# Masked keys by strided transfers through DRAM in every stacked attention

## The chip, the cores and the metric

One of the cores of a Trainium2 chip runs the whole program; seven stand idle. The metric is the device time in microseconds of one execution, the median of three. The engines, as the profile names them: PE multiplies matrices (PEld loads its weights), DVE, ACT and POOL work on vectors, SP only issues transfers. DMA engines, 16 for the core, carry the transfers, and semaphores order everything.

## The reference

`x` is 64 sequences of 128 tokens of width 128; the context has 120 tokens per sequence. Four layers, each a cross attention and a feed-forward block:

```python
x = x + _L0_xattn_ref(_layernorm(x), ctx, ctx, pad, ...)     # a0: every 4th key per head
x = x + _L0_ffn_ref(_layernorm(x), ...)                      # f0
x = x + _L1_xattn_ref(_layernorm(x), ctx, wq, bq, ...)       # a1: plain
x = x + _L1_ffn_ref(_layernorm(x), ...)                      # f1
x = x + _L2_xattn_ref(_layernorm(x), ctx, ctx, mask, ...)    # a2: mask; routing for f2 beside it
x = x + _L2_ffn_ref(_layernorm(x), ...)                      # f2
x = x + _L3_xattn_ref(_layernorm(x), ctx, ctx, ...)          # a3: causal, no biases
x = x + _L3_ffn_ref(_layernorm(x), ...)                      # s3 and f3
# inside _L3_ffn_ref:
h = layernorm(x, ln1_scale, ln1_shift)
x = x + attention(h, wq, wk, wv, wo, bo)                     # s3: causal self attention, 128 keys
```

Every attention has 16 heads of width 8:

```python
q = (x_q @ wq + bq); k = (x_kv @ wk + bk); v = (x_kv @ wv + bv)    # split into 16 heads
scores = einsum('bhqd,bhkd->bhqk', q, k) / sqrt(8)
out = einsum('bhqk,bhkd->bhqd', softmax(scores + mask), v) @ wo + bo
```

## The kernel before

`attention_phase` is called once per attention (a0, a1, a2, a3, s3). The trace calls the tiles of a0 to a3 `a_...` and those of s3 `s_...`. A block works on 16 groups of four sequences. All but a0 are "packed" (stacked): 16 slots per group, slot = 4 x sequence + unit, where a unit is four heads. In a slot PE multiplies 96 rows of stacked queries with 96 rows of stacked, masked keys into scores for four heads (L1276; in a2, a3 and s3 the mask is added by L1282), DVE takes the row maxima (L991) and subtracts them (L996), ACT takes the exponential (L1172). Three slots later PE turns the result (L1291), ACT copies it (L1178), and four to six slots later PE multiplies it with the values (L1315), DVE inverts the sums and normalises (L1004, L1010), PE applies Wo (L1330). PE takes its work in the order of the program: scores of the slot, what is behind, and in some slots a projection for the next group (`slot_of`: keys in slot 0, normalised rows 4, queries 7 or 8, values 13; in s3, whose keys come out of its own rows, rows 1, keys 4, queries 8, values 13).

"Stacked" means three float32r terms for full precision: the keys as high, low, high part in partitions 0 to 31, 32 to 63, 64 to 95 (32 dimensions of one unit each), the queries as high, high, low. "Masked" means: the unit's four heads share these 32 dimensions, so the keys stand four times side by side, each copy with zeros in the dimensions of the three other heads. The way of the keys of a group through a1, a3 and s3: PE projects them (L1245), ACT evicts them (L1164 or L1166) and rounds the high part (`high_part`, L1130), POOL subtracts for the low part (`low_part`, L882), SP stacks them by twelve transfers of 32 partitions into K3 (`stack_terms`, L791), POOL multiplies each of the four units of K3 with `slots`, the 0/1 table of heads (`masked_keys`, L723), into KM. The queries then go by twelve transfers into QR (L797). SP issues in order, and after the keys it waits for the low part of the queries. PE waits for each unit's KM and QR in the slots of the first sequence (`scores`).

a2 goes another way: `place_keys` writes the three terms to the DRAM tensor `stacked_keys` (L805), SP waits until they are there (`keys_kept`), and four strided reads (L812) put each head's eight dimensions at their places in a KM whose zeros were written once at the start (L911) and by group 0's masked keys; then `stack_queries` (L821). Its Wk, Wq and biases are brought into another order of dimensions at the start of the block: weights by ACT (`reorder`, L1117), biases by transfers (`dims_first`, L696).

There are two KM and two QR, one K3, one high and one low part for keys and queries.

Of the kernel before, what the change touches and what calls it, by code (L numbers as in the profile page):

```python
# [22 lines left out]
P = 128  # L23
D = 128
# [563 lines left out]
def attention_phase(nc, R, I, name, wq, wk, wv, wo, bq=None, bk=None, bv=None, bo=None, hepos=False,  # L588
# [20 lines left out]
    with ExitStack() as stack:  # L609
# [63 lines left out]
        if packed:  # L673
# [3 lines left out]
            q3_in = [sem(n_(f"q3_in{i}")) for i in range(4)]  # L677
        if route:
            keys_kept, keys_empty, keys_in = (sem(n_(s)) for s in ("keys_kept", "keys_empty", "keys_in"))
            reordered = sem(n_("reordered"))  # L680
# [6 lines left out]
        n_weights += 3 * bool(route)  # L687
        n_weights += 2 * (ln is not None) + hepos
# [3 lines left out]
        def dims_first(eng, col, bias, there):  # L692

            by_dim = bias.rearrange("(i j r a) -> i r j a", i=4, j=4, a=1)
            for i in range(4):
                eng.dma_start(cols[32 * i:32 * i + 32, col:col + 1], by_dim[i],  # L696
                              allow_slow_non_contiguous=True).then_inc(there, 16)

# [34 lines left out]
        with nc.Block() as block:  # L733
            @block.sync
            def _(sp):
# [4 lines left out]

                sp.dma_start(PT[0][:, 0:D] if route else Wk[:], wk).then_inc(keys_first_in, 16)
                if not route:
                    if bk is not None:
                        sp.dma_start(cols[:, 1:2], bk.rearrange("(p a) -> p a", a=1)).then_inc(keys_first_in, 16)
                    sp.dma_start(slots[:], I["slots" if packed else "slot_classes"]).then_inc(keys_first_in, 16)
                if not own_keys:
                    ctx_load(0, 0)
                for t, w in ((PT[0][:, D:2 * D] if route else Wq[:], wq), (Wv[:], wv), (Wo[:], wo)):
                    sp.dma_start(t, w).then_inc(weights_in, 16)
                if route:  # L750
                    dims_first(sp, 0, bq, weights_in)
                for c, v in ((0, None if route else bq),) + (((3, ln[0]), (4, ln[1])) if ln else ()):
                    if v is not None:
                        sp.dma_start(cols[:, c:c + 1], v.rearrange("(p a) -> p a", a=1)).then_inc(weights_in, 16)
# [17 lines left out]
                def stack_first():  # L772
# [7 lines left out]
                    for i in (2, 3):  # L780
                        for term, part in enumerate((HIGH, HIGH, LOW)):
                            sp.dma_start(QR[0][32 * term:32 * term + 32, i, :].bitcast(F32),
                                         part["q"][32 * i:32 * i + 32, :].bitcast(F32)).then_inc(q3_in[i], 16)

                def stack_terms(g, par):
# [7 lines left out]
                    sp.wait_ge(low_ready["q"], g + 1)  # L793
                    for i in range(4):
                        at_least(sp, sc_ready, (g - 2) * S + (GB - 1) * U + i + 1)
                        for term, part in enumerate((HIGH, HIGH, LOW)):
                            sp.dma_start(QR[par][32 * term:32 * term + 32, i, :].bitcast(F32),  # L797
                                         part["q"][32 * i:32 * i + 32, :].bitcast(F32)).then_inc(q3_in[i], 16)

                def place_keys(g, par):  # L800

                    sp.wait_ge(low_ready["k"], g + 1)
                    for term, part in enumerate((HIGH, LOW, HIGH)):
                        kept = R.keys.rearrange("(t q i f) -> t i q f", t=3, q=32, i=4)[term]
                        sp.dma_start(kept, part["k"][:].bitcast(F32)).then_inc(keys_kept, 16)  # L805
# [4 lines left out]
                    of_head = R.keys.rearrange("(q j s k) -> j q s k", q=24, j=4, k=KN)  # L810
# [4 lines left out]
                def stack_queries(g, par):  # L815
# [13 lines left out]
                if own_keys:  # L829
                    groups_loop(sp, lambda g, par, first, last: stack_first() if first else stack_terms(g, par), 3)  # L830
                    return
# [8 lines left out]
                stack_first()  # L840
                if route:
                    for g in range(1, NG):
                        if g + 1 < NG:
                            ctx_load(g + 1, (g + 1) % 2)
                        place_keys(g, g % 2)
                        stack_queries(g, g % 2)
                    return

                def pair(g):
                    ctx_load(g + 2, 0)  # L850
                    stack_terms(g + 1, 1)
                    ctx_load(g + 3, 1)
                    stack_terms(g + 2, 0)

                pairs_loop(sp, NG - 2, pair)
                stack_terms(NG - 1, 1)

            @block.gpsimd
            def _(pool):
# [32 lines left out]
                def prepare(g, par):  # L892
                    low_part("k", g)
                    if not route:
                        masked_keys(pool, nc.gpsimd, g, par, (0,))
                    scatter(g - 1, 4, 7)
                    low_part("q", g)
                    if not route:
                        masked_keys(pool, nc.gpsimd, g, par, (1, 2, 3))
                    scatter(g - 1, 15, 3)  # L900
# [7 lines left out]
                low_part("k", 0)  # L908
                masked_keys(pool, nc.gpsimd, 0, 0, (0, 2))
                if route:  # L910
                    nc.gpsimd.memset(KM[1][:].bitcast(F32), 0.0).then_inc(keys_empty, 1)  # L911
                    route.spares()
# [192 lines left out]
            def _(act):  # L1105
                a = nc.scalar
                if route:
                    dims_first(act, 1, bk, keys_first_in)
                    by_dim = I["slots"].rearrange("(t j r) w -> t r j w", t=3, j=4)
# [10 lines left out]

                if route:
                    reorder(Wk, 0)
# [75 lines left out]
                for step in steps_of:  # L1198
                    if step == "v" and bv is None:
                        act.wait_ge(prep_pool, 2)  # L1200
                    if step == ("ht" if own_keys else "q"):
                        act.wait_ge(weights_in, 16 * n_weights)
                        at_least(act, prep, n_prep)
                    if route and step == "ht":
                        act.wait_ge(weights_in, 16 * n_weights)
                        reorder(Wq, 1)
# [16 lines left out]
            def _(pe):  # L1223
# [140 lines left out]

                if route:
                    pe.wait_ge(reordered, 1)
# [6 lines left out]
                for step in steps_of[1:]:  # L1373
                    if route and step == "q":
                        pe.wait_ge(reordered, 2)
# [1261 lines left out]
def build(nc, I, out):  # L2637
    with ExitStack() as stack:
# [9 lines left out]
        R.dispatched = nc.dram_tensor("dispatched", [E2 * CAP + 2 * NB * P, ROW], F32).ap()  # L2648
        R.keys = nc.dram_tensor("stacked_keys", [3 * P * GB * KC], F32).ap()
        R.chosen = nc.dram_tensor("chosen", [2 * NB * P + SPARE, D], F32).ap()  # L2650
# [115 lines left out]
```

## Time and profile before

| | us |
|---|---|
| median of 3 runs | 4092.15 |
| lowest, highest | 4079.58, 4092.81 |
| the profiled execution, device time | 4094.84 |
| its span in the trace | 4093.0 |
| PE, DVE, ACT, POOL busy | 3449.9, 3381.5, 2376.4, 1347.5 |
| granted TensorE clock, mean | 0.912 |

The blocks with stacked attention stand at about 549 to 990 us (a1), 1372 to 1965 (a2), 2407 to 2890 (a3) and 2911 to 3430 (s3). The profile is of one execution. A share of busy time over the span mixes stages; a row of one stage says more. "Idle before" is the time for which the engine had nothing to do before the instructions of a group, with what ended it. The duration of a transfer issue (SPq) is only the issue; the landing is seen in the DMA share or in who waited for it.

### The profile page before, as it was taken

What the parts mean: (1) busy time and instruction counts of PE and PEld (TensorE: products, weight loads), DVE (VectorE), ACT (ScalarE), POOL (GpSimd) and SP (SyncE); (2) the same over time, 40 slices, a digit from 0 to 9 for tenths busy, and PEclk for the clock granted to TensorE, in tenths of its full rate; (3) what the DMA queues carried; (4) which work ended last, traced back from release to release, by engine and by line L of the source; (5) the groups of instructions that cost most, each with busy time, mean ns of one, the idle gap of its engine ahead of it and who ended that gap; (6) DMA issues with size and microseconds to landing.
All of it is one profiled execution on the core that took longest, in us unless ns stands there. A gap on an engine that the chain in (4) does not pass through costs nothing. (4 is left out here: it accounts for less than half of the span.)

```text
span 4093.0 us, 94365 instructions
## 1 busy us (share of the span) xinstructions
PE 3449.9 (84%) x31907; PEld 2493.3 (61%) x31907; DVE 3381.5 (83%) x6484; ACT 2376.4 (58%) x4442; POOL 1347.5 (33%) x876
## 2 busy tenths in 40 slices
PE   6983979999499698888568839999499998899999
PEld 3543647676477465566446627777366666677777
DVE  7888879999799798777655569999788887788888
ACT  2431647777277466666545527777567664566665
POOL 1210025554000202222344435564255552122222
PEclk9995979999599799999789869999699997899999
DMA  2001312221100133332122142222222222000000
GB/s 65 14 23 54 145 45 68 62 65 44 55 1 0 43 86 79 79 81 73 46 85 61 57 127 64 65 67 52 76 48 54 55 50 83 18 16 15 15 11 15
DMA packets 182176, 221.18 MB, mean 54 GB/s; under 512 B 59144, under 2 KB 131148, under 8 KB 178957
## 3 DMA queue, kind: packets, MB, share of 16 engines
q1 hardware_dynamic: 172277, 198.88, 17.8%
q0 software_dynamic: 8192, 16.92, 1.5%
q8 instruction: 189, 3.10, 0.3%
q10 hardware_dynamic: 1432, 1.58, 0.2%
q14 instruction: 86, 0.70, 0.1%
HBM read 64.15 MB, written 53.26 MB: 29 GB/s over the span
## 5 line engine op out<-in xcount | busy, mean ns | idle before, releaser
L1172 ACT ACTIVATE a_p<-a_p 128x480 f32<-128x480 f32 x832 | 501.6, 603 | 453.9 <-DVE a_p L996 442.8
L991 DVE TENSOR_REDUCE a_mx<-a_sc 128x4 f32<-128x480 f32 (+1 forms) x832 | 539.9, 649 | 142.4 <-PE a_sc L1282 89.1
L1178 ACT ACTIVATE a_pt<-a_tp 120x512 f32<-120x512 f32 x832 | 485.3, 584 | 110.7 <-PE a_tp L1291 102.9
L996 DVE TENSOR_TENSOR a_p<-a_sc,a_mx 128x480 f32<-128x480 f32 x832 | 531.0, 638 | 19.7 <-DVE a_mx L991 0.5
L1291 PE MATMUL a_tp<-ident,a_p 128*120 128x128 f32 x3328 | 516.7, 278 | 19.3 <-issue 12.0
L1291 PEld LDWEIGHTS a_tp<-ident,a_p 128*120 128x120 f32 x3328 | 411.0, 140 | 98.6 <-issue 51.0
L723 POOL TENSOR_TENSOR a_km<-a_k,a_slots 96x1920 fp32r<-96x1920 f32 x126 | 426.6, 3405 | 133.3 <-DMA a_k<-a_kh 133.3
L1276 PE MATMUL a_sc<-a_km,a_qr 96*128 96x480 f32 x768 | 401.1, 522 | 64.6 <-DVE a_p L996 48.8
L1315 PE MATMUL a_nd<-a_pt,a_vm 120*32 120x128 f32 x6656 | 304.4, 286 | 27.4 <-ACT a_pt L1178 24.6
L2276 ACT ACTIVATE f_s<-f_pu 128x512 f32<-128x512 f32 x256 | 153.3, 599 | 214.0 <-PE f_pv L1758 214.0
L1315 PE MATMUL a_nd<-a_pt,a_dm 120*32 120x128 f32 x6656 | 271.0, 276 | 1.1 <-issue 1.1
L1276 PEld LDWEIGHTS a_sc<-a_km,a_qr 96*128 96x128 f32 x768 | 148.2, 193 | 170.8 <-issue 95.8
L1004 DVE RECIPROCAL a_rd<-a_nd 128x128 f32<-128x128 f32 x256 | 242.5, 947 | 10.6 <-PE a_nd L1315 10.3
L723 POOL TENSOR_TENSOR s_km<-s_k,s_slots 96x2048 fp32r<-96x2048 f32 x62 | 223.6, 3625 | 55.2 <-DMA s_k<-s_kh 55.2
L1172 ACT ACTIVATE s_p<-s_p 128x512 f32<-128x512 f32 x256 | 161.2, 630 | 138.2 <-DVE s_p L996 138.0
L2187 DVE TENSOR_TENSOR f_a<-f_s,f_pv 128x512 f32<-128x512 f32 x256 | 175.2, 685 | 77.4 <-ACT f_s L2276 70.7
L1315 PEld LDWEIGHTS a_nd<-a_pt,a_vm 120*32 120x32 f32 x6656 | 146.8, 110 | 143.0 <-issue 71.4
L2199 DVE TENSOR_TENSOR f_al<-f_a,f_ah 128x512 fp32r<-128x512 f32 x256 | 228.9, 894 | 0.0
L2162 POOL TENSOR_TENSOR f_ya<-f_ya,f_yg 128x512 f32<-128x512 f32 x96 | 124.8, 1300 | 302.7 <-DVE f_yg L2212 302.5
L991 DVE TENSOR_REDUCE s_mx<-s_sc 128x4 f32<-128x512 f32 x256 | 175.0, 684 | 44.7 <-PE s_sc L1282 43.4
L1282 PE MATMUL a_sc<-a_addm,ident_bf 128*128 128x480 bf16 x512 | 199.7, 390 | 0.7 <-issue 0.7
L1315 PEld LDWEIGHTS a_nd<-a_pt,a_dm 120*32 120x32 f32 x6656 | 195.8, 112 | 3.2 <-issue 2.5
(458 smaller groups left out, 8796.1 us busy)
## 6 DMA issues: line engine op xcount, KB each, us to landing
a_qr<-a_qh SPq DMA_DIRECT2D x372, 64.0 KB, 2.0
a_k<-a_kh SPq DMA_DIRECT2D x264, 60.0 KB, 2.0
a_ctx<-in_ctxT SPq DMA_DIRECT2D x64, 240.0 KB, 2.7
a_qr<-a_ql SPq DMA_DIRECT2D x186, 64.0 KB, 2.0
a_km<-stacked_keys SPq DMA_DIRECT2D x60, 180.0 KB
dispatched<-f_empty SPq DMA_DIRECT2D x8, 1040.0 KB, 20.0
f_xr<-dispatched SPq DMA_DIRECT2D x32, 260.0 KB, 2.6
chosen<-f_none SPq DMA_DIRECT2D x8, 1024.0 KB, 11.9
```

The lines of the kernel that those rows point to most:

```text
L723: v.tensor_tensor(KM[par][:, i, :, :].rearrange("p b (j k) -> p b j k", k=KN), K3[:, i, :, :].unsqueeze(2).to_broadcast([TR, GB, 4, KN]), ...
L991: v.tensor_reduce(mx[:], view, AX.X, ALU.max).then_inc(mx_ready, 1)
L996: v.tensor_tensor(PR[s % 4][:].rearrange("p (h k) -> p h k", k=k), view, mx[:].unsqueeze(2).to_broadcast([P, heads, k]), ALU.subtract).the ...
L1004: v.reciprocal(RD[:], ND[bt % 2][:, 1, :]).then_inc(rd_ready, 1)
L1172: a.activation(PR[s % 4][:], PR[s % 4][:], ACT.Exp).then_inc(exp_ready, 1)
L1178: a.activation(PT[s % 4][0:KN, :], TP[s % 2][0:KN, :], ACT.Copy).then_inc(pt_ready, 1)
L1276: last = t.matmul(SC[s % 2][:, 0:W], queries, keys, start=True, stop=not masked)
L1282: last = t.matmul(SC[s % 2][:, 0:W], R.ident_bf[:], addm[:].unsqueeze(1).to_broadcast([P, 4, KN]), start=False, stop=True)
L1291: last = t.transpose(TP[s % 2][0:KN, q * P:(q + 1) * P], PR[s % 4][:, q * KN:(q + 1) * KN], R.ident[:])
L1315: last = t.matmul(ND[j % 2][32 * q:32 * q + 32, what, :], w, PT[s % 4][0:KN, q * P:(q + 1) * P], start=(what == 0 and i == 0), stop=(i == ...
L2187: v.tensor_tensor(A[s % 2][:], S[s % 2][:], PV[s % 2][:], ALU.mult).then_inc(Z["a_ready"], 1)
L2199: v.tensor_tensor(AL[s % 4][:], A[s % 2][:], AH[s % 4][:].bitcast(F32), ALU.subtract).then_inc(Z["lo_ready"], 1)
```

## The change

a1, a3 and s3 go a2's way. `stack_terms` now holds what `place_keys` did, for all; SP's loops are written out in full; POOL no longer runs `masked_keys` after group 0 but clears KM[1] once; PE waits for one count of four reads in slot 0 instead of four counts; weights, biases and slots are loaded and reordered as in a2; `stacked_keys` grows so that it holds 128 keys. a0, a2 and the feed-forward blocks stay.

```diff
-        n_first = 8 if route else 2 + (bk is not None)
+        n_first = 2 + (bk is not None) if hepos else 4 + 4 * (bk is not None)
...
         def parts_free(eng, step, g):
-            if route and step == "k" and g > 1:
-                eng.wait_ge(keys_kept, 48 * (g - 1))
+            if step == "k" and isinstance(g, int) and g == 1:
+                for i in range(4):
+                    eng.wait_ge(k3_in[i], 48)
+            elif step == "k":
+                at_least(eng, keys_kept, 48 * (g - 1))
             else:
                 for i in range(4):
-                    at_least(eng, (k3_in if step == "k" else q3_in)[i], 48 * g)
+                    at_least(eng, q3_in[i], 48 * g)
...
                 def stack_terms(g, par):
                     sp.wait_ge(low_ready["k"], g + 1)
-                    for i in range(4):
-                        at_least(sp, km_ready[i], g)
-                        for term, part in enumerate((HIGH, LOW, HIGH)):
-                            sp.dma_start(K3[32 * term:32 * term + 32, i, :, :].rearrange("p b k -> p (b k)"),
-                                         part["k"][32 * i:32 * i + 32, :].bitcast(F32)).then_inc(k3_in[i], 16)
+                    for term, part in enumerate((HIGH, LOW, HIGH)):
+                        sp.dma_start(kept_keys[term].rearrange("q (i f) -> i q f", i=4),
+                                     part["k"][:].bitcast(F32)).then_inc(keys_kept, 16)
+                    sp.wait_ge(keys_kept, 48 * g)
+                    if par == 1:
+                        sp.wait_ge(keys_empty, 1)
+                    at_least(sp, sc_ready, (g - 1) * S)
+                    for j in range(4):
+                        sp.dma_start(KM[par][j:TR:4, :, :, j * KN:(j + 1) * KN].bitcast(F32),
+                                     of_head[j]).then_inc(keys_in, 16)
                     sp.wait_ge(low_ready["q"], g + 1)
...
                 def prepare(g, par):
                     low_part("k", g)
-                    if not route:
-                        masked_keys(pool, nc.gpsimd, g, par, (0,))
                     scatter(g - 1, 4, 7)
                     low_part("q", g)
-                    if not route:
-                        masked_keys(pool, nc.gpsimd, g, par, (1, 2, 3))
                     scatter(g - 1, 15, 3)
...
                 masked_keys(pool, nc.gpsimd, 0, 0, (0, 2))
+                nc.gpsimd.memset(KM[1][:].bitcast(F32), 0.0).then_inc(keys_empty, 1)
...
                     if packed and j == 0:
-                        if not route or g == 0:
-                            pe.wait_ge(km_ready[i], g + 1)
+                        if isinstance(g, int) and g == 0:
+                            pe.wait_ge(km_ready[i], 1)
                         elif i == 0:
                             pe.wait_ge(keys_in, 64 * g)
                         pe.wait_ge(q3_in[i], 48 * (g + 1))
```

The order on SP in s3, one group, before (s_k is K3, s_kh and s_kl the high and low part of the keys, s_qr the stacked queries):

```order
L791 DMA s_k<-s_kh 32x512
L791 DMA s_k<-s_kl 32x512
L791 DMA s_k<-s_kh 32x512 x2
L791 DMA s_k<-s_kl 32x512
L791 DMA s_k<-s_kh 32x512 x2
L791 DMA s_k<-s_kl 32x512
L791 DMA s_k<-s_kh 32x512 x2
L791 DMA s_k<-s_kl 32x512
L791 DMA s_k<-s_kh 32x512
L797 DMA s_qr<-s_qh 32x512 x2
```

The same place now (stacked_keys is the DRAM tensor, s_km the masked keys):

```order
L793 DMA stacked_keys<-s_kh 4x32x512
L793 DMA stacked_keys<-s_kl 4x32x512
L793 DMA stacked_keys<-s_kh 4x32x512
L800 DMA s_km<-stacked_keys 24x16x128 x4
L806 DMA s_qr<-s_qh 32x512 x2
L806 DMA s_qr<-s_ql 32x512
```

Between the third and the fourth row SP now waits for the three writes, and the first query transfer stands behind the four reads.

The order on POOL in s3 at the start of the block, before (s_ql is the low part of the queries):

```order
L882 TENSOR_TENSOR s_kl<-s_kt,s_kh 128x512
L723 TENSOR_TENSOR s_km<-s_k,s_slots 96x2048 x2
L882 TENSOR_TENSOR s_kl<-s_kt,s_kh 128x512
L723 TENSOR_TENSOR s_km<-s_k,s_slots 96x2048
L882 TENSOR_TENSOR s_ql<-s_qt,s_qh 128x512
L723 TENSOR_TENSOR s_km<-s_k,s_slots 96x2048 x3
```

And now:

```order
L855 TENSOR_TENSOR s_kl<-s_kt,s_kh 128x512
L724 TENSOR_TENSOR s_km<-s_k,s_slots 96x2048 x2
L879 MEMSET s_km 96x8192
L855 TENSOR_TENSOR s_kl<-s_kt,s_kh 128x512
L855 TENSOR_TENSOR s_ql<-s_qt,s_qh 128x512
```

After group 0 only the two low parts stand on POOL, and one clearing of KM[1] ahead of them.

## Rows read from the trace of the kernel before

**Rows 1.** busy time by stage: a1, a3, s3; the first row names the columns
```profile
core 0: us, PE busy (x) PEld busy (x) DVE busy (x) ACT busy (x) POOL busy (x), PEclk, DMA share, GB/s
600.00:985.00 385.00, 365.25 (x5032) 269.66 (x5021) 367.41 (x697) 281.47 (x518) 221.47 (x85) 1.00 0.26 64
2440.00:2880.00 440.00, 437.08 (x5942) 317.02 (x5938) 401.74 (x763) 320.80 (x592) 235.10 (x89) 1.00 0.25 60
2970.00:3400.00 430.00, 407.80 (x5279) 288.14 (x5279) 385.03 (x685) 296.08 (x533) 234.94 (x84) 1.00 0.22 53
```

**Rows 2.** what PE waited for in s3: us in total, times, longest
```profile
PE s_pj L1238 <- DVE s_h L157: 19.0, 14, 2.0
```

**Rows 3.** groups of s3, a3 and a2: busy us, mean ns, idle before
```profile
L723 POOL TENSOR_TENSOR s_km<-s_k,s_slots 96x2048 fp32r<-96x2048 f32 x54 | 193.3, 3597 | 48.2 <-DMA s_k<-s_kh 48.2
L157 DVE TENSOR_SCALAR s_h<-x,s_mean,s_rstd 128x128 f32 x52 | 27.7, 591 | 0.0
...
L996 DVE TENSOR_TENSOR a_p<-a_sc,a_mx 128x480 f32<-128x480 f32 x149 | 94.5, 634 | 1.9
...
L996 DVE TENSOR_TENSOR a_p<-a_sc,a_mx 128x480 f32<-128x480 f32 x193 | 123.1, 638 | 2.8 <-issue 0.3
```

**Rows 4.** L157 in s3: ns shortest, median, longest
```profile
L157 DVE TENSOR_SCALAR s_h<-x,s_mean,s_rstd x52: 332/334/1952, 2998.7 to 3370.1; 128x128 f32 x52
```

**Rows 5.** SP in a2 by start; two stretches of it; landing (us)
```profile
1446.07 0.59 SPq L805 DMA_DIRECT2D stacked_keys<-a_kh  x1
1457.08 3.26 SPq L812 DMA_DIRECT2D a_km<-stacked_keys  x4
1460.45 1.23 SPq L821 DMA_DIRECT2D a_qr<-a_qh  x2
1468.04 0.59 SPq L821 DMA_DIRECT2D a_qr<-a_ql  x1
...
1453.00:1454.00 1.00, 1.00 (x30) 0.66 (x22) 1.00 (x3) 0.98 (x2) 0.00 (x0) 1.00 0.26 102
1465.00:1466.00 1.00, 1.00 (x8) 0.78 (x7) 0.98 (x2) 0.00 (x0) 0.00 (x0) 1.00 0.18 41
...
a_qr<-a_ql SPq DMA_DIRECT2D x186, 64.0 KB, 2.0
```

**Rows 6.** s3 by start: SP, POOL, PE (scores of slots 0, 3, 4)
```profile
2980.98 0.51 SPq L791 DMA_DIRECT2D s_k<-s_kh  x1
3011.55 0.52 SPq L791 DMA_DIRECT2D s_k<-s_kh  x1
...
2984.25 3.60 POOL L723 TENSOR_TENSOR s_km<-s_k,s_slots 96x2048 fp32r<-96x2048 f32 x1 [3.30 <-DMA s_k<-s_kh]
...
2996.41 0.50 PE L1276 MATMUL s_sc<-s_km,s_qr 96*128 96x512 f32 x1
3002.76 0.47 PE L1276 MATMUL s_sc<-s_km,s_qr 96*128 96x512 f32 x1
3005.28 0.49 PE L1276 MATMUL s_sc<-s_km,s_qr 96*128 96x512 f32 x1
```

**Rows 7.** a1: SP's first key transfer, PE's scores of slots 0 and 3
```profile
613.11 0.51 SPq L791 DMA_DIRECT2D a_k<-a_kh  x1
...
634.73 0.49 PE L1276 MATMUL a_sc<-a_km,a_qr 96*128 96x480 f32 x1
639.24 0.49 PE L1276 MATMUL a_sc<-a_km,a_qr 96*128 96x480 f32 x1
```

**Rows 8.** a2, two stretches of 10 us
```profile
1650.00:1660.00 10.00, 6.39 (x66) 3.65 (x64) 6.44 (x21) 7.01 (x16) 6.35 (x8) 0.99 0.37 77
1660.00:1670.00 10.00, 9.78 (x87) 6.54 (x84) 8.44 (x23) 6.65 (x14) 1.95 (x2) 0.67 0.45 116
```

**Rows 9.** start of a2: SP's transfers of the query bias
```profile
1374.56 3.08 SPq L696 DMA_DIRECT2D a_cols<-in_L_xattn_b_q  x4
```

**Rows 10.** a2: a wait of DVE that nothing in the profile released
```profile
1659.55 0.66 DVE L991 TENSOR_REDUCE a_mx<-a_sc 128x4 f32<-128x480 f32 x1 [3.25 <-remote]
```

More of the change, by code:

```diff
@@ L683, in attention_phase @@
         rd_ready, ct_ready, o_done, x_added = (sem(n_(s)) for s in ("rd_ready", "ct_ready", "o_done", "x_added"))
-        n_first = 8 if route else 2 + (bk is not None)
+        n_first = 2 + (bk is not None) if hepos else 4 + 4 * (bk is not None)
         n_weights = 3 + sum(a is not None for a in (bq, bo, mask, causal, pad)) + (GB if bv is not None else 0)
-        n_weights += 3 * bool(route)
+        n_weights += 3 * (packed and bq is not None)
         n_weights += 2 * (ln is not None) + hepos
@@ L695, in dims_first @@
             for i in range(4):
-                eng.dma_start(cols[32 * i:32 * i + 32, col:col + 1], by_dim[i],
-                              allow_slow_non_contiguous=True).then_inc(there, 16)
+                eng.dma_start(cols[32 * i:32 * i + 32, col:col + 1], by_dim[i], allow_slow_non_contiguous=True).then_inc(there, 16)
         def class_keys(pool, g, par):
@@ L739, in ctx_load @@
                     sp.dma_start(CTX[par][:], I["ctxT"][:, bass.ds(g * GB, GB), :]).then_inc(ctx_in[par], 16)
-                sp.dma_start(PT[0][:, 0:D] if route else Wk[:], wk).then_inc(keys_first_in, 16)
-                if not route:
+                sp.dma_start(PT[0][:, 0:D] if packed else Wk[:], wk).then_inc(keys_first_in, 16)
+                if hepos:
                     if bk is not None:
                         sp.dma_start(cols[:, 1:2], bk.rearrange("(p a) -> p a", a=1)).then_inc(keys_first_in, 16)
-                    sp.dma_start(slots[:], I["slots" if packed else "slot_classes"]).then_inc(keys_first_in, 16)
+                    sp.dma_start(slots[:], I["slot_classes"]).then_inc(keys_first_in, 16)
                 if not own_keys:
                     ctx_load(0, 0)
-                for t, w in ((PT[0][:, D:2 * D] if route else Wq[:], wq), (Wv[:], wv), (Wo[:], wo)):
+                for t, w in ((PT[0][:, D:2 * D] if packed else Wq[:], wq), (Wv[:], wv), (Wo[:], wo)):
                     sp.dma_start(t, w).then_inc(weights_in, 16)
-                if route:
+                if packed and bq is not None:
                     dims_first(sp, 0, bq, weights_in)
-                for c, v in ((0, None if route else bq),) + (((3, ln[0]), (4, ln[1])) if ln else ()):
+                for c, v in ((0, bq if hepos else None),) + (((3, ln[0]), (4, ln[1])) if ln else ()):
                     if v is not None:
@@ L783, in stack_first @@
                                          part["q"][32 * i:32 * i + 32, :].bitcast(F32)).then_inc(q3_in[i], 16)
+                kept_keys = R.keys[0:3 * P * GB * KN].rearrange("(t q s) -> t q s", t=3, q=32)
+                of_head = R.keys[0:3 * P * GB * KN].rearrange("(q j s k) -> j q s k", q=24, j=4, k=KN)
                 def stack_terms(g, par):
                     sp.wait_ge(low_ready["k"], g + 1)
-                    for i in range(4):
-                        at_least(sp, km_ready[i], g)
-                        for term, part in enumerate((HIGH, LOW, HIGH)):
-                            sp.dma_start(K3[32 * term:32 * term + 32, i, :, :].rearrange("p b k -> p (b k)"),
-                                         part["k"][32 * i:32 * i + 32, :].bitcast(F32)).then_inc(k3_in[i], 16)
[L793 to L802, printed above, removed]
                     for term, part in enumerate((HIGH, LOW, HIGH)):
-                        kept = R.keys.rearrange("(t q i f) -> t i q f", t=3, q=32, i=4)[term]
-                        sp.dma_start(kept, part["k"][:].bitcast(F32)).then_inc(keys_kept, 16)
+                        sp.dma_start(kept_keys[term].rearrange("q (i f) -> i q f", i=4),
+                                     part["k"][:].bitcast(F32)).then_inc(keys_kept, 16)
                     sp.wait_ge(keys_kept, 48 * g)
@@ L829, in _ @@
                 if own_keys:
-                    groups_loop(sp, lambda g, par, first, last: stack_first() if first else stack_terms(g, par), 3)
+                    groups_in_full(lambda g, par, first, last: stack_first() if first else stack_terms(g, par))
                     return
@@ L840, in _ @@
                 stack_first()
[L841 to L856, printed above, removed]
+                for g in range(1, NG):
+                    if g + 1 < NG:
+                        ctx_load(g + 1, (g + 1) % 2)
+                    stack_terms(g, g % 2)
             @block.gpsimd
@@ L1106, in _ @@
                 a = nc.scalar
-                if route:
-                    dims_first(act, 1, bk, keys_first_in)
+                if packed:
+                    if bk is not None:
+                        dims_first(act, 1, bk, keys_first_in)
                     by_dim = I["slots"].rearrange("(t j r) w -> t r j w", t=3, j=4)
@@ L1203, in _ @@
                         at_least(act, prep, n_prep)
-                    if route and step == "ht":
+                    if packed and step == "ht":
                         act.wait_ge(weights_in, 16 * n_weights)
@@ L1363, in group @@
                             behind(g, s, par, False)
-                if route:
+                if packed:
                     pe.wait_ge(reordered, 1)
@@ L1373, in _ @@
                 for step in steps_of[1:]:
-                    if route and step == "q":
+                    if packed and step == "q":
                         pe.wait_ge(reordered, 2)
@@ L2648, in build @@
         R.dispatched = nc.dram_tensor("dispatched", [E2 * CAP + 2 * NB * P, ROW], F32).ap()
-        R.keys = nc.dram_tensor("stacked_keys", [3 * P * GB * KC], F32).ap()
+        R.keys = nc.dram_tensor("stacked_keys", [3 * P * GB * P], F32).ap()
         R.chosen = nc.dram_tensor("chosen", [2 * NB * P + SPARE, D], F32).ap()
```

7 lines of the change are left out of this document (1 added, 6 removed).

## The prediction

> **What bounds the kernel now.** I read the busy time by stage first, then the waits, then single groups. A group is four batches, sixteen slots, and each block has 16 groups. In the block a1 (600 to 985 us), the causal block a3 (2440 to 2880) and the self attention s3 (2970 to 3400) PE is busy 365.25 of 385, 437.08 of 440 and 407.80 of 430 us at the full clock, and POOL 221 to 235 us [rows 1]. So these blocks go at TensorE's pace, and POOL, whose work the change takes away, has about 45% of its time free. What matters is whether anything waits for POOL. In s3 the one large wait of PE is for the normalised rows, 19.0 us in 14 groups [rows 2]; none of PE's waits names the masked keys. Hence the removed work can pay only by what it does to other engines, and the added transfers cost only by when they land.
>
> **What is removed.** Per group of a1, a3 and s3: four POOL multiplications, in s3 3597 ns each [rows 3], 14.4 us; in 45 groups about 640 us of POOL. They lie beside PE work and are worth nothing by themselves. Twelve small SP transfers into K3 per group go too. Do they slow DVE? The subtraction L996 takes 634 ns in a3 beside a busy POOL and 638 in a2, which has no masked keys on POOL [rows 3]: no. Only L157 (SBUF to SBUF, one tensor) shows it: 591 ns on the mean in s3, while its fastest and its median are 332 and 334 [rows 3, 4]. In a1 and a3 its slow ones stand at slots 1 and 2, beside POOL's low part of the keys, which stays; PE is 95 to 99% busy there, and I count 0. In s3 they stand in slot 0, beside the last masked keys, and PE waits behind them. Gain there: 4 x (591 - 332) = 1.0 us of PE's 1.36 us (19.0 / 14) per group.
>
> The Trainium skill (GPSIMD Engine Reference, the table at its head) says that GpSimd and VectorE share SBUF interfaces and collide for DVE instructions in a two-port mode or with two SBUF inputs. By that rule also POOL's four multiplications would have cost DVE only at L157, where the trace has it, so an engine that is freed on this scale brings the softmax nothing; a reader who expects the 640 us of POOL to come back in part is told no by both.
>
> **What is added.** Per group: three writes of the stacked keys to DRAM, a wait for them, four strided reads into KM, and only then the twelve query transfers, since all stand on SP's one queue. a2 does exactly this now (slot 0 as a1, 480 values a row), so its rows give the times. From the first write to the first read 11.0 us (1446.07 to 1457.08), while the 16 DMA engines are busy 0.26: about four of them carry it; in the groups at 1502 and 1538 it is 10.8, and I take that. From the first read to the first query transfer 3.37 us, to the last query transfer 10.96 us. Traffic is down to 0.18 of the engines at 1465, 8 us after the first read, with six query transfers in it; I take keys and the first unit's queries as landed 7.4 us after the first read [rows 5]. The floor is 3.37 + 3.3 = 6.7 us, the 3.3 being what three stacked transfers take now from first issue to use, 2980.98 to 2984.25 [rows 6].
>
> **In a1 and a3** the keys are projected in slot 0. The first transfer goes out at 613.11 and the next group's first scores start at 634.73, 21.6 us later [rows 7]. The new chain needs 10.8 + 7.4 = 18.2 us. 3.4 us are left, and the queries of unit 3 (10.8 + 10.96 + 2.0 to land = 23.8 us) are wanted three slots later, at 639.24, 26.1 us. So 0 for these 30 group changes, bounded by a few us of either sign.
>
> **In s3** the keys are projected in slot 4, since they come out of the group's own rows. First transfer 2980.98, next group's first scores 2996.41: 15.4 us, and the same again 30.57 us on [rows 6]. The new chain: 10.8 us, plus 0.5 because 512 instead of 480 values per row take 1/15 more of some 7.4 us of moving, plus 7.4: 18.7 us. PE reaches slot 0 and waits 3.3 us. Everything in PE's order stands behind it (the turns and values of the previous group, the projection of ht), and DVE and ACT run dry after their queue. Then the queries of units 1 to 3 come behind: the last lands 10.96 + 2.0 = 13.0 us after the first read, so slot 3 starts no sooner than 5.6 us after slot 0, and slot 4 2.5 us later (3002.76 to 3005.28), 8.1 us in all. Before it is 8.87 us (2996.41 to 3005.28), PE's wait for L157 inside, so 0.8 us come back here and that gain is used up. Net +2.5 us per group. Bounds: chain 11.3 + 6.7 with L157's whole gain, 18.0 - 15.4 - 1.2 = +1.4; and 12.0 + 7.8 with nothing back, +4.4. With 15 group changes: +37 us (21 to 66).
>
> **The clock.** In a2 five stretches of 10 us with PE busy 6.4 to 7.1 were each followed by one with the granted clock at 0.66 to 0.83, as at 1650 and 1660 [rows 8]. A wait of 3.3 us plus thinner slots gives about 6.5 of 10. One such fall costs (1 - 0.73) x 10 = 2.7 us of full-speed work. What falls on slots 0 to 4 lengthens the group; what falls later only fills the wait. I take under half, 1.2 us: 15 x 1.2 = +18 (0 to 40).
>
> **Start of the blocks.** Weights come unordered and ACT reorders them; biases come in four transfers, slots in three. a2 shows the price: SP's four bias transfers take 3.08 us [rows 9], one about a seventh of it (0.43). In a1 the scores hang on SP's list (bias vectors, bo, then keys), longer by 3.08 less three issues of 0.43: +1.8. In a3 the slots land 1 us after what gates the first projection now: +1. In s3 the norm covers it: 0. The clearing of KM[1] on POOL (one pass over a buffer, by size at most two of the 3.6 us multiplications) stands before the next low part and delays it by about 1 us, where 3.4 us are left. Sum +3 (1 to 8).
>
> **Sum.** The profiled execution took 4094.84 us. 4094.84 + 37 + 18 + 3 = 4153; it lies 2.7 us above the median of the runs, so 4150.
>
> The Trainium skill (DMA: Bandwidth & Descriptors, Specifications) wants pieces of at least 512 bytes and says that below this the DMA reads, modifies and writes. The pieces of a1, a2 and a3 are 120 x 4 = 480 bytes, those of s3 128 x 4 = 512. By it the reads in s3 land sooner than a2's 7.4 us; the issue of the queries (6.7 us) then decides, and the whole would be 0.7 x 15 = 10 us less, 4140. No row before the change has a 512-byte read of this form.
>
> **Rivals.**
> (A) The keys come in time in s3 too: faster. It decides at 15.4 us from first write to last landing; L157's gain of 1.0 us then stays, 15 x 1.0, less 3 at the starts: 4080. For it: s3 has no indirect transfers beside, and PE's waits in a2 name no key. Against: the write alone took 10.8 us in a2's first groups, where there were none either, and a2 has over 21 us.
> (B) The small gains and losses cancel, the landing being just late: 4092. The chain would have to be 2.5 us shorter than in a2.
> (C) Instructions run short. In a2 DVE stood 3.25 us at 1659.55 with its input ready since 1656.3, and PE's transposes came one by one, all during the write to DRAM [rows 10]. It shows in 5 of a2's 15 writes, each with indirect transfers beside. If a third of the writes of a3 and s3 did it: 10 x 3.2 on top, 4182; in all 45 groups +144, 4294. Against: a2's first writes, without indirect transfers, have nothing of it.
> (D) The chain is late in a1 and a3 also. The margin is 3.4 us; each us beyond costs 30 us: 4180. Against: a2 has the same order at hardly more room, and none of PE's waits there names the keys.
>
> **Chances.** Forecast (s3 late, the rest hidden) 0.79, its own range 4115 to 4180; A 0.08; B 0.04; C 0.06; D 0.03. 0.3% is 12 us, about what a measurement here can tell. Faster: A with a little of B, 0.08; within 0.3%: B and the lowest edge of the forecast, 0.06; slower 0.86. The range, 4108 to 4182, leaves out most of A and B and the upper part of C.
>
> **What would show it.** Right: in s3 PE waits about 3 us at each group's first scores, released by a DMA into s_km or s_qr; the group takes 33 to 34.5 us instead of 30.57; the granted clock of s3 falls below 0.97; a1 and a3 keep 27.6 and 27.9 us per group; L157 in s3 nears 0.34 us; POOL is under 20% busy in the three blocks. Wrong: if s3 keeps 30.6 us or less (A), if PE or DVE show idle time that nothing released (C), or if the time between first write and first read in s3 is not 11.3 us.

## The result, and the profile after

The changed kernel takes 4155.8 us (median of 4 executions, 4152.3 to 4159.8), the kernel before beside it 4092.5. The ratio is 1.016, its 95% interval 1.013 to 1.019. The forecast was 4150, range 4108 to 4182, slower with 0.86. The profiled execution took 4152.3, its span is 4150.5.

The lengths of the blocks show where the time went. Each is counted from the first weight transfer of its attention, in us of the span:

| stretch | before | after | difference |
|---|---|---|---|
| a1 and its feed-forward block | 822.6 | 825.7 | +3.1 |
| a2 and its feed-forward block | 1035.6 | 1032.2 | -3.3 |
| a3 up to the start of s3 | 503.5 | 504.8 | +1.3 |
| s3, to its last output product | 518.2 | 576.8 | +58.6 |

The busy time by stage, three rows that answer to [rows 1]; columns: stretch, its length, busy us and instructions of PE, PEld, DVE, ACT, POOL, the granted clock, the DMA share and GB/s:

```profile
600.00:985.00 385.00, 364.70 (x5043) 269.28 (x5043) 365.48 (x695) 281.03 (x516) 34.81 (x28) 1.00 0.34 90
2440.00:2880.00 440.00, 434.24 (x5933) 316.33 (x5931) 400.36 (x764) 320.38 (x590) 36.11 (x29) 1.00 0.32 85
2970.00:3400.00 430.00, 380.36 (x4711) 273.05 (x4711) 331.53 (x614) 265.86 (x475) 31.93 (x25) 0.92 0.26 70
```

POOL falls from 221 to 235 us to 32 to 36 in all three. In a1 and a3 PE, DVE and ACT keep their busy time and the clock stays at full speed: freeing POOL brings nothing. In s3 PE is busy for less of the same 430 us (380.36 against 407.80), at a mean granted clock of 0.92.

What PE waited for in s3 between 2970 and 3400 us, answering to [rows 2]: the wait for L157 is gone, and in its place stands the wait for the masked keys, 3.8 us a time.

```profile
PE s_sc L1246 <- DMA s_km<-stacked_keys: 49.8, 13, 5.0
```

L157 itself, answering to [rows 3, 4], takes 317 ns on the mean instead of 591 now that POOL is free, and its longest is 346 ns instead of 1952:

```profile
L157 DVE TENSOR_SCALAR s_h<-x,s_mean,s_rstd x52: 245/340/346, 2976.1 to 3387.2; 128x128 f32 x52
```

One group of s3, SP and then PE by start time, answering to [rows 5, 6]. The columns are start, duration and instruction, in brackets the wait before it. The PE lines are the scores of slots 0, 1 and 4:

```profile
2989.12 0.58 SPq L793 DMA_DIRECT2D stacked_keys<-s_kh  x1
3000.48 3.26 SPq L800 DMA_DIRECT2D s_km<-stacked_keys  x4
3003.84 1.24 SPq L806 DMA_DIRECT2D s_qr<-s_qh  x2
...
3008.29 0.77 PE L1246 MATMUL s_sc<-s_km,s_qr 96*128 96x512 f32 x1 [3.66 <-DMA s_km<-stacked_keys]
3010.02 0.77 PE L1246 MATMUL s_sc<-s_km,s_qr 96*128 96x512 f32 x1
...
3017.52 0.50 PE L1246 MATMUL s_sc<-s_km,s_qr 96*128 96x512 f32 x1
```

From the first write to the first read it is 11.36 us, from there to the scores of slot 0 7.81, and from slot 0 to slot 4 9.23. The first scores take 0.77 us instead of 0.5. Single microseconds around them show why (columns as above):

```profile
2993.00:2994.00 1.00, 1.00 (x34) 0.80 (x33) 1.00 (x3) 1.00 (x2) 0.00 (x0) 1.00 0.26 100
3006.00:3007.00 1.00, 0.00 (x0) 0.00 (x0) 0.00 (x0) 0.00 (x0) 0.00 (x0) 1.00 0.61 154
3007.00:3008.00 1.00, 0.00 (x0) 0.00 (x0) 0.00 (x0) 0.00 (x0) 0.00 (x0) 0.53 0.56 149
3012.00:3013.00 1.00, 1.00 (x21) 0.91 (x24) 1.00 (x3) 0.33 (x1) 0.00 (x0) 0.50 0.55 129
3015.00:3016.00 1.00, 1.00 (x10) 0.77 (x8) 0.84 (x2) 0.52 (x2) 0.00 (x0) 1.00 0.00 0
```

The first row lies in the write to DRAM, at a DMA share of 0.26. In the second and third all five engines stand. The granted clock falls to 0.5 (1.2 of 2.4 GHz) before the wait is over, and is full again by 3015.

In s3 the keys of fifteen groups are prepared in this way, and slot 0 of all fifteen waits. The means over the 13 of them that lie between 2970 and 3400 us, by the same four marks, with the same 13 before:

| us per group | before, one group [rows 6] | before, mean | after, mean |
|---|---|---|---|
| first transfer to first read | | | 11.33 |
| first read to scores of slot 0 | | | 8.04 (7.66 to 9.19) |
| the two, or first transfer to scores of slot 0 | 15.43 | 15.43 | 19.37 |
| slot 0 to slot 4 | 8.87 | 9.10 (8.85 to 10.54) | 8.68 |
| slot 4 to the next first transfer | 6.27 | 6.27 | 6.10 |
| group | 30.57 | 30.80 | 34.16 |

The group of [rows 6] is one of the short ones: four groups before are longer, up to 32.24 us. So a group grows by 3.4 us on the mean and not by 3.6.

The +58.6 us of s3 have three parts. From the first of the fifteen key transfers to the last it is 430.98 us before and 479.33 after, fourteen groups at 3.45 us more: +48.4. From the last one to the last output product it is +6.1, with the last late arrival in it (4.1) and slots 0 to 4 of the last group, 8.52 us instead of 6.49. The third part is +4.1 between the start of the block and the first of these transfers, and it has nothing to do with late keys. It stands in the first group, beside the clearing of KM[1] on POOL. POOL, then DVE, then PE after the change, and below them the same DVE and PE rows before:

```profile
2936.37 7.00 POOL L879 MEMSET s_km<- 96x8192 f32 x1
2939.10 4.92 DVE L157 TENSOR_SCALAR s_h<-x,s_mean,s_rstd 128x128 f32<-128x128 f32 x4
2944.17 1.09 PE L1208 MATMUL s_pj<-ident,s_h 128*128 128x128 f32 x4 [9.90 <-DVE s_h L157]
...
2939.48 1.10 DVE L157 TENSOR_SCALAR s_h<-x,s_mean,s_rstd 128x128 f32<-128x128 f32 x4
2940.73 1.08 PE L1238 MATMUL s_pj<-ident,s_h 128*128 128x128 f32 x4 [6.08 <-DVE s_h L157]
```

The first two of the four L157 take 4.35 and 4.16 us instead of 0.33 and end within 0.15 us of the clearing; the other two take 0.33 us. In a1 the clearing, from 578.00 to 584.49, has the same neighbour: an L157 that starts at 581.81 takes 2.76 us and ends at 584.57. In s3 PE waits 9.90 us for these L157 instead of 6.08, and slot 2 of the first group starts 34.7 us after the start of the block instead of 30.6.

### The profile page after: what moved, and what is told of

Same layout as the page of the kernel before. It is cut to its first block and busy times, and to the rows that moved or that the text cites. A ratio compares the mean times of both kernels' runs of the same rounds, so it can differ in the third digit from the quotient of the medians.

```text
span 4150.5 us, 93531 instructions
## 1 busy us (share of the span) xinstructions
PE 3458.4 (83%) x31907; PEld 2507.4 (60%) x31907; DVE 3370.6 (81%) x6484; ACT 2382.2 (57%) x4448; POOL 751.2 (18%) x699
## 3 DMA queue, kind: packets, MB, share of 16 engines
q10 hardware_dynamic: 1952, 1.58, 0.2%
## 5 line engine op out<-in xcount | busy, mean ns | idle before, releaser
L973 DVE RECIPROCAL a_rd<-a_nd 128x128 f32<-128x128 f32 x256 | 242.5, 947 | 10.6 <-PE a_nd L1285 10.3
L1148 ACT ACTIVATE s_pt<-s_tp 128x512 f32<-128x512 f32 x256 | 149.9, 586 | 80.8 <-PE s_tp L1261 78.7
L1246 PE MATMUL s_sc<-s_km,s_qr 96*128 96x512 f32 x256 | 141.6, 553 | 62.3 <-DMA s_km<-stacked_keys 57.3
L1724 PE MATMUL f_py<-f_ah,f_wdhi 128*128 128x512 f32 x384 | 181.7, 473 | 0.0
```

What stands on the lines that cost most here:

```text
L973: v.reciprocal(RD[:], ND[bt % 2][:, 1, :]).then_inc(rd_ready, 1)
L1148: a.activation(PT[s % 4][0:KN, :], TP[s % 2][0:KN, :], ACT.Copy).then_inc(pt_ready, 1)
L1246: last = t.matmul(SC[s % 2][:, 0:W], queries, keys, start=True, stop=not masked)
L1724: t.matmul(out, w_hi, a_hi, start=start, stop=False)
```

## The experiments

Each kernel is told by its edit of the changed kernel, if nothing else is said; the diffs are shortened. The ratio is to the kernel before, timed on the same chip, with its 95% interval. Means per group are over the 13 groups of s3 between 2970 and 3400 us where nothing else is said.

**e1: s3 back on K3 and POOL, a1 and a3 changed.**

```diff
+                    if own_keys:
+                        for i in range(4):
+                            at_least(sp, km_ready[i], g)
+                            for term, part in enumerate((HIGH, LOW, HIGH)):
+                                sp.dma_start(K3[32 * term:32 * term + 32, i, :, :].rearrange("p b k -> p (b k)"),
...
```

> The changed kernel with the self attention s3 back on K3 and POOL's multiplications; a1 and a3 stay on the way through DRAM, as do the new loads at the starts of all blocks. Theory (keys land late in s3 alone): the loss is gone, group of s3 back at 30.6 us, 4096 (4088 to 4104). Rival 1 (a1 and a3 carry part of the loss, by their DMA traffic or instruction supply): 4110 or more. Rival 2 (the freed POOL pays in a1 and a3 and s3 only covers it up): below 4085.

4098.8 us, ratio 1.0008 (0.9994 to 1.0022); s3 519.4 us, groups of 30.84. PE waits for L157 as it did:

```profile
PE s_pj L1223 <- DVE s_h L157: 18.4, 13, 2.0
```

So the loss stands in s3, and e1 is as expected. What a1 and a3 pay at their starts is inside this interval. With K3 back, s3 has no clearing either: its first four L157 take 1.10 us together, and slot 2 of its first group starts 30.8 us after the start of the block. In every kernel here that clears KM[1] in s3 it is 34.7 to 35.0 us. No run moves the clearing alone.

**e3 and e8: s3's keys projected one slot later (5), one slot earlier (3).**

```diff
-    slot_of = dict(zip(steps_of, ... (1, 4, 8, 13)))
+    slot_of = dict(zip(steps_of, ... (1, 5, 8, 13)))
```

e8 has 3 in the place of 5.

> The changed kernel with s3's keys projected in slot 5 instead of slot 4, one slot or 1.5 to 1.9 us later. Theory: the wait grows by the same, from 3.7 to 5.4 us, in 15 group changes: +23 to +29, and up to 10 more by the clock: 4179 to 4195. Rival (wait independent of the slot): 4156.

> The changed kernel with s3's keys projected in slot 3 instead of 4, 2.5 us earlier; the eviction of ht, for which slot 2 had to wait 1.36 us, is over by then. Theory: wait of PE for the keys 1.2 us, no fall of the clock: group 30.5 to 30.8, 4094 to 4102. Rival (slot 2's group of 30.66 us is a floor set by something else than ht): the same 30.66 with another wait.

e3: 4179.1, ratio 1.0202 (1.0169 to 1.0236), groups of 35.45 us. The way through DRAM is as long as in the changed kernel (11.32 and 7.86 us); slot 4 to the next first write takes 7.51 instead of 6.10, and the wait grows from 3.8 to 4.70, not quite to the 5.4 expected. e8: 4114.2, ratio 1.0045 (1.0030 to 1.0061), groups of 31.43 where slot 0 still waits (11.33 and 8.13, then 8.63 and 3.34):

```profile
PE s_sc L1246 <- DMA s_km<-stacked_keys: 17.9, 12, 2.1
```

The time follows the distance between projection and first use, as a late arrival demands. e8 missed its expectation of 4094 to 4102. The wait is 1.5 us on the mean and not 1.2, the clock does fall a little (0.98 in the row of the stage), and a group that waits for no key takes 29.73 us (e7 below), where the expected 30.5 to 30.8 leaves 29.3 to 29.6 for it.

**e2: the keys in slot 2.**

```diff
-    slot_of = dict(zip(steps_of, ... (1, 4, 8, 13)))
+    slot_of = dict(zip(steps_of, ... (1, 2, 8, 13)))
```

> The changed kernel with s3's keys projected in slot 2 instead of slot 4, 3.9 us earlier in a group. Theory: PE's wait of 3.7 us at slot 0 shrinks to under 0.5 us, the clock stays at 1.00, and L157's gain shows: group 29.6 to 30.6 us, 4088 to 4103. Rival (the wait is not a matter of how early the keys are asked for, but of the reads or of contention at slot 0): wait and time stay, about 4150.

4105.4, ratio 1.0030 (1.0014 to 1.0047), groups of 30.66 us, granted clock 1.00. No wait for the keys is left, but another one:

```profile
PE s_pj L1215 <- ACT s_ht L1115: 19.0, 14, 1.4
```

The projection now stands one slot behind the turn of the rows it needs, and waits for ACT's copy of them: 1.36 us per group, as much as L157 cost before the change. With it e2 lies a little above its expected 4088 to 4103. A fixed order of PE has a late limit and an early one.

**e5: the wait filled with fourteen matmuls whose result is not used** (all else as in the changed kernel).

```diff
+                    if own_keys and s == 0 and g > 0:
+                        pe.wait_ge(ready["v"], g + 1)
+                        for _ in range(FILLERS):
+                            t.matmul(PJ[:], R.ident_bf[:], addm[:].unsqueeze(1).to_broadcast([P, 4, KN]), start=True,
+                                     stop=True)
```

> The changed kernel with 14 matmuls of 512 columns (bf16, 0.22 us each at full clock, results unused) on PE ahead of s3's first scores of each group, that is inside the wait. Theory (the fall of the clock is a cost of its own, 1.2 us per group): the granted clock of s3 stays near 1.00, the wait row shrinks to 0.6 us, the group goes from 34.1 to 32.9 us, 4138. Rival (what the clock takes is hidden by the wait for the keys anyway): clock back, group still 34.1, 4156. Rival (the fillers themselves delay): above 4160.

4145.1, ratio 1.0122 (1.0089 to 1.0155); s3 566.5 us instead of 576.8, groups of 33.59 instead of 34.16. The row of the stage has the full clock (its PE time contains the fillers):

```profile
2970.00:3400.00 430.00, 410.49 (x4992) 278.41 (x4987) 337.66 (x625) 268.79 (x485) 31.96 (x25) 1.00 0.27 71
```

PE by start time, the fillers and then the scores of slots 0, 2 and 4:

```profile
3008.08 3.20 PE L1236 MATMUL s_pj<-s_addm,ident_bf 128*128 128x512 bf16 x14
3011.68 0.47 PE L1252 MATMUL s_sc<-s_km,s_qr 96*128 96x512 f32 x1 [0.40 <-issue]
...
3016.50 0.50 PE L1252 MATMUL s_sc<-s_km,s_qr 96*128 96x512 f32 x1 [0.19 <-DMA s_qr<-s_ql]
...
3019.75 0.50 PE L1252 MATMUL s_sc<-s_km,s_qr 96*128 96x512 f32 x1
```

Slot 0 to slot 4 takes 7.93 us here on the mean (8.07 in this group) against 8.68: the low clock costs 0.75 us there, 11 us in 15 groups. In all it is 10.3 us by the length of s3, 10.7 by the medians and 14 by the two ratios. The keys come no sooner than without the fillers: slot 0 starts 8.25 us after the first read on the mean (8.04 without them), and 8.45 in the eight groups in which PE is seen to wait for them after the fillers. So the late arrival and not the clock is the cause; the clock is its smaller consequence.

**e4: in s3 the queries ahead of the wait for the writes.**

```diff
+                    if own_keys:
+                        queries(g, par)
                     sp.wait_ge(keys_kept, 48 * g)
```

> The changed kernel with s3's twelve query transfers issued while SP would wait for the writes, ahead of the four reads. Theory: the queries are ready 6 to 7 us after the first write, so the reads start at about 14 instead of 11.4 us, but then nothing stands behind them, slots 1 to 3 are not held back, and the reads land sooner than 7.8 us after their start: 6 us gives a landing at 20 against 19.2 us. Sum near zero, 4145 to 4175. Rival (the queries in the queue are what holds the reads back): landing at 14 + 4.5, a gain, below 4145.

4208.8, ratio 1.0270 (1.0247 to 1.0293), groups of 37.5: a miss, by more than 30 us. `queries` is the wait for the low part and the twelve query transfers. One group by start time, SP and then PE:

```profile
3040.08 0.55 SPq L793 DMA_DIRECT2D stacked_keys<-s_kh  x1
3047.49 1.89 SPq L813 DMA_DIRECT2D s_qr<-s_qh  x2
...
3055.82 3.31 SPq L802 DMA_DIRECT2D s_km<-stacked_keys  x4
...
3062.69 0.79 PE L1253 MATMUL s_sc<-s_km,s_qr 96*128 96x512 f32 x1 [7.02 <-DMA s_km<-stacked_keys]
```

SP's wait for the low part of the queries ends only 7.4 us after the first write; POOL makes it at 3046.19. The twelve issues then take 8.3 us, and the reads start 15.9 us after the first write on the mean instead of 11.3. Less than half of the query transfers fits into the wait for the write. The run has a side result: with no query transfer behind the reads, the keys land 6.69 us after the first read (6.42 to 6.96, 13 groups) instead of 8.04. So the queries issued behind the reads hold the reads up by about 1.3 us, at least by this one comparison.

**e6: s3's three writes of 128 rows as twelve of 32 rows.**

```diff
-                        sp.dma_start(kept_keys[term].rearrange("q (i f) -> i q f", i=4),
-                                     part["k"][:].bitcast(F32)).then_inc(keys_kept, 16)
...
+                        for i in range(4):
+                            sp.dma_start(kept_keys[term].rearrange("q (i f) -> i q f", i=4)[i],
+                                         part["k"][32 * i:32 * i + 32, :].bitcast(F32)).then_inc(keys_kept, 16)
```

> The changed kernel with s3's three writes to DRAM cut into twelve of 32 rows each, so that each can go out on all 16 DMA engines instead of 4. Theory (the write of 11.4 us is long because four engines carry it): issue of twelve at 0.63 us is 7.6 us and 2 us to land, 9.6 us from first write to first read; the wait of PE goes from 3.7 to 2.0 us, with part of the clock's cost: 15 x 1.7 to 2.4, so 4120 to 4132. Rival (the write is bound by something else, DRAM or the receipt): still 11 us or more, 4150 to 4165.

4095.1, ratio 0.9998 (0.9987 to 1.0009), groups of 30.06: better than the 4120 to 4132 expected. SP by start time:

```profile
2993.16 2.63 SPq L798 DMA_DIRECT2D stacked_keys<-s_kh  x4
3000.85 3.31 SPq L805 DMA_DIRECT2D s_km<-stacked_keys  x4
```

One microsecond inside the write:

```profile
2997.00:2998.00 1.00, 1.00 (x33) 0.81 (x32) 1.00 (x3) 0.97 (x2) 0.00 (x0) 1.00 0.54 135
```

First write to first read is 7.69 us in this group and 7.59 on the mean (6.79 to 8.08) instead of 11.33, at a DMA share of 0.54 instead of 0.26. It is now mostly SP's own issuing, which takes 6.4 us in this group. With 3.7 us off the chain the keys come nearly in time: PE still stands 0.5 us on the mean before slot 0 (up to 1.5), which the profile puts down to nothing. The gain at L157 is seen: the group is 0.7 us shorter than before the change (30.06 against 30.80).

The Trainium skill (DMA: Bandwidth & Descriptors, Why a DMA increments its semaphore by 16 and not by 1) states that a transfer is spread over the largest number of engines, up to 16, that divides the slowest dimension of both its sides. By it a write in the form 4x32x512 goes to four engines, a share of 0.25, and one of 32 rows to sixteen. The trace agrees with 0.26 for the first; for the second its 0.54 shows over twice as much as four engines can give, and not that it is sixteen.

**e7: both, slot 3 and twelve writes in s3.** The two diffs above together.

> Slot 3 and the twelve writes together. Theory: the keys land 0.5 us or more before PE reaches slot 0, no wait of PE in s3 is left over 1 us, and DVE's L157 is fast: group 29.2 to 29.8 us, 15 x 1.0 below the kernel before, less 4 for the starts of the blocks: ratio 0.997, 4080 to 4090. Rival (freeing POOL brings s3 nothing): group 30.5, ratio 1.001.

4090.7, ratio 0.9985 (0.9973 to 0.9996), s3 508.6 us, groups of 29.73. No wait of PE between 2970 and 3400 us is above 0.3 us any more:

```profile
PE s_pj L1213 <- DVE s_h L157: 4.5, 14, 0.3
PE s_nd L1290 <- ACT s_pt L1153: 3.2, 14, 0.2
```

The row of the stage, where [rows 1] had 407.80 us of PE:

```profile
2970.00:3400.00 430.00, 421.76 (x5478) 298.19 (x5472) 380.04 (x706) 306.84 (x550) 35.87 (x28) 1.00 0.33 82
```

The groups are as expected; the time lies just above the expected 4080 to 4090. It took 4 us off for the starts of the blocks, and they cost more: a1 with its feed-forward block is 3.2 us longer than before, a3 2.4, and s3 pays the 4.1 us beside the clearing here too.

**e9: as e7, and a1 and a3 back on K3 and POOL.**

```diff
+    direct = packed and (bool(route) or own_keys)
...
-                if packed:
+                if direct:
```

> Only the self attention s3 (and a2 as before) takes the way through DRAM, with its keys projected in slot 3 and its write cut into twelve transfers of 32 rows; a1 and a3 are back on K3 and POOL. My theory (the way through DRAM brings a1 and a3 nothing and costs about 3 us at their starts): s3 about 509 us as in the kernel with slot 3 and twelve writes in s3, a1 from start to start back by about 3 us, the whole 4086 at a before of 4092, ratio 0.9975. Rival (the start of a1 costs nothing, or what POOL leaves free in a1 and a3 is worth as much as the start costs): ratio 0.9985 like that kernel. Second rival (POOL's freedom in a1 and a3 is worth more than the start): ratio 0.9995 or above.

4082.8, ratio 0.9974 (0.9965 to 0.9982), as expected. a1 with its feed-forward block takes 821.6 us against 825.8 in e7, a3 504.2 against 505.9: the starts.

**e10: as e9, and a2's writes in twelve too; e11: the changed kernel with slot 3 and twelve writes in all four blocks.** The diff is e10 against e9:

```diff
-                        if not own_keys:
+                        if False:
```

This is the branch of e6 that keeps three writes outside s3.

> As the kernel with the way through DRAM in s3 and a2 only, and a2's write is cut into twelve transfers of 32 rows too. Tests rival (C): a2's stalls with nothing to release them, five of about 3 us, come from its three writes, which four DMA engines carry. If so, they go, and it is 10 to 16 us faster than that kernel, ratio about 0.994. If they come from the indirect transfers beside, or from transfers in general, a2 stays at its 1035 us with its feed-forward block and the ratio is 0.9975.

> The changed kernel with s3's keys in slot 3 and all writes of all four blocks cut into twelve transfers of 32 rows. My theory: in a1 and a3 the write was hidden, so twelve writes bring nothing there; SP issues nine more transfers per group there but has the time; ratio as for the kernel with slot 3 and twelve writes in s3 alone, 0.9985, a1 and a3 groups at 27.6 and 27.9 us. Rival (the write by four engines slows a1 or a3 a little, or stalls a2): up to 15 us less, ratio 0.995. Rival (more transfers on SP's queue delay the queries): slower than that kernel by 5 us or more.

e10: 4073.9, ratio 0.9956 (0.9941 to 0.9971), the fastest of all. e11: 4082.5, ratio 0.9971 (0.9958 to 0.9983), where 0.9985 was expected; its a1 (826.2 us) and a3 (507.8) still pay for the way through DRAM. The interval of e10 just overlaps that of e9, and the traces say where the gain is. a2 with its feed-forward block takes 1023.0 us in e10 and 1025.0 in e11; in the eleven traces whose a2 has three writes it takes 1029.8 to 1041.7. a2's groups beside the indirect transfers take 41.4 and 37.0 us by turns before (medians of five each) and 41.1 and 37.2 in e9, and they take 40.2 and 36.0 in e10. The waits with nothing to release them, though, are still there (before: [rows 10]). In e9:

```profile
1657.18 0.66 DVE L981 TENSOR_REDUCE a_mx<-a_sc 128x4 f32<-128x480 f32 x1 [3.13 <-remote]
```

And in e10:

```profile
1657.52 0.66 DVE L981 TENSOR_REDUCE a_mx<-a_sc 128x4 f32<-128x480 f32 x1 [2.90 <-remote]
```

They stand in every group from the sixth on at the same instruction, ten in e9 and nine in e10 (the profile puts the first one there down to PE), and are shorter by 0.25 us. So the expectation that they go with the three writes failed, and so did its alternative that a2 keeps its length. The write by four engines does not make these waits; what does stays open. That a shorter write makes a2's groups about 1.1 us faster is measured; by what chain was not followed.

## Why the prediction was right

**Where, and by what.** The trace and e1 put the loss in s3 alone, e3, e8 and e6 move it with the distance between projection, landing and use, and e5 takes the clock out without taking the wait out. That is the mechanism forecast. Rivals A and B (in time, or just late) fall with the 49.8 us of wait. D falls with a1 and a3, whose groups from the second on take 27.62 and 27.90 us on the mean (27.58 and 27.87 before). C falls too: once the blocks are under way, neither PE nor DVE has a wait of over 0.5 us in a1, a3 or s3 that nothing in the profile released. C counted five such waits in a2 before; the trace has ten, five of 3.1 to 3.3 us and five of 2.6.

**The chain in s3.** Write 11.3 forecast, 11.33 measured. Landing 7.4 forecast, 8.04 measured: the forecast read it off a stretch in which the DMA share had fallen, not off a wait that ended, and e4 shows the share that the queries behind it have in it. Late by 3.3 forecast, by 3.94 measured (19.37 less 15.43). What comes back was put too low as well. At the full clock slots 0 to 4 take 7.93 us (e5), where the forecast had 8.1, and before the change they take 9.10 on the mean, where it had one group's 8.87; another 0.17 comes back after them. So without the clock a group costs 3.94 - 1.17 - 0.17 = 2.6 us, and 2.5 was forecast.

**The clock.** Of the term of 18 us e5 finds about 11, 0.75 us per group and not 1.2. The fall begins in the wait already, so that a part of the low clock costs nothing, and the queries gate slots 0 to 4 in part, as the short wait for s_qr at 3016.50 in e5 shows. The two terms together, 55 forecast, measure 48.4 + 6.1 = 54.5. That they meet so closely is partly luck: the lateness was put 0.6 us too low, what comes back 0.5 us too low and the clock 0.45 us too high per group, and the last group, which gives nothing back, costs 6.1.

**The starts.** +3 forecast, too low. a1's scores start 2.2 us later (+1.8 forecast), a3's 1.5 (+1 forecast). For s3 the forecast had 0 and is wrong: it has +4.1 us. The forecast saw the clearing of KM[1] only as a delay of POOL's next low part; what it holds up is DVE's L157 beside it, and PE's turn of those rows stands ahead of the scores of slot 2. With +3.1 in a1's stretch and +1.3 in a3's the three make +8.5. e7 against e9 gives 4.2 and 1.7 for a1 and a3, and about 4.5 for both by the ratios. a2, unchanged in its code, is 3.3 us shorter in the profiled execution, which covers part of it; its length varies from 1029.8 to 1041.7 us between traces that leave it alone, so this is scatter and luck.

**L157 and POOL.** 1.36 us of wait per group gone and 591 ns fallen to 317, as forecast; DVE's subtraction keeps its time in s3 (673 ns mean after). 14 us of POOL per group bring a1 and a3 nothing, and s3 only this one wait, which shows as a gain only where the keys are in time or nearly so (e6, e7). The forecast had seen that POOL slows L157 and had not applied it to its own clearing at the start of s3.

**The pieces of 512 bytes.** The prediction drew on the Trainium skill (DMA: Bandwidth & Descriptors, Specifications): by it the reads of s3, in pieces of 512 bytes, would have landed sooner than a2's in pieces of 480, for 4140 us. They land 8.04 us after the first read, where 7.4 was read off a2. The trace doesn't bear out a gain at this size. It isn't a clean comparison, since the 7.4 is itself an estimate from a DMA share; of the 8.04, e4 puts about 1.3 down to what stands behind the reads on the queue.

## What to carry to other kernels

Taking work off an engine with half its time free is worth what waits for it, here one wait of 1.4 us per group; the way that replaces it must be timed from projection to first use, and compared with the slots in between, block by block: the same edit cost under 0.1 us per group in a1 and a3 and 3.4 in s3. Look at the DMA share during a transfer on which others wait: 0.26 says that few engines carry it, and cutting it so that more do (e6, ratio 0.9998) was worth more than moving the work by a slot (e8, 1.0045). When an order is written out by hand, move the projection together with the change (e7, e10). And look at what one-time work at a block's start stands beside: clearing a buffer once on an engine with time to spare cost 4.1 us, as much as three of the waits for L157 that the change removes.

## What was not expected

Twelve writes of 32 rows land in 7.6 us from first issue, three of 128 rows with the same bytes in 11.3. Query transfers queued behind the reads delay the reads that stand ahead of them, 8.04 instead of 6.69 us. The granted clock is down in the row at 3007, in which PE still stands, and full again in the row at 3015: part of the slow time costs nothing. A clearing on POOL of 7.0 us holds a DVE instruction of 0.33 us for 4.35 us, until the clearing ends; the forecast had no term for it.
